# Moving the value projection behind the query-key transposes, and giving the self-attention output another PSUM bank, in a two-layer decoder kernel

## What is computed

```python
h = layernorm(x) * ln_g + ln_b                 # xn, then xT once it is transposed
q, k, v = h @ Wq.T, h @ Wk.T, h @ Wv.T         # 4 heads of 64
q, k = rmsnorm(q) * q_gamma, rmsnorm(k) * k_gamma
p = softmax(q @ k.T / 8)                       # per head
x1 = layernorm(layernorm(x) + (p @ v) @ Wo.T + bo)
```

## Time and profile before

| | |
|---|---|
| Median of 3 runs | 1514.06 us (1513.68 to 1515.25) |
| Profiled execution | 1514.06 us, span 1512.2 us |
| Mean granted clock of PE | 0.956 of full |
| Busy share of the span: PE, DVE, ACT, POOL | 90%, 73%, 62%, 55% |
| Self-attention stage (to slot 63) | about the first 160 us |
| Cross-attention stage | to about 650 us |

### The profile page before, as it was taken

One profiled execution on the slowest core, in us unless ns is written; L12 is line 12 of the kernel. 1 busy time (PEld: TensorE's weight loads), 2 busy tenths in 40 slices (PEclk: granted clock), 3 DMA queues, 4 the chain that ended last, 5 costly groups with the idle time before them and its releaser, 6 DMA issues.

```text
span 1512.2 us, 27707 instructions
## 1 busy us (share of the span) xinstructions
PE 1355.4 (90%) x9290; PEld 1093.8 (72%) x9290; DVE 1110.2 (73%) x2430; ACT 930.7 (62%) x2302; POOL 830.5 (55%) x866
## 2 busy tenths in 40 slices
PE   4888999999999999956999999878899998999991
PEld 4666777777777777645899999734556565899991
DVE  4898766666666766646688886389898996779935
ACT  4776565555655556534488884147788883548853
POOL 3675454444444444431688875138796885048850
PEclk9999999999999999975899999979999999999996
DMA  4100000000000000034566657674444340227784
GB/s 153 43 29 8 29 9 8 2 8 2 8 9 1 9 1 1 2 120 183 191 230 228 226 210 233 231 267 136 143 155 145 129 140 14 96 85 250 260 270 177
DMA packets 52942, 167.85 MB, mean 111 GB/s; under 512 B 13178, under 2 KB 22340, under 8 KB 44996
## 3 DMA queue, kind: packets, MB, share of 16 engines
q1 hardware_dynamic: 45316, 145.63, 27.3%
q0 software_dynamic: 7488, 20.46, 4.2%
HBM read 149.28 MB, written 16.78 MB: 110 GB/s over the span
## 4 chain that ended last, share of the span: by engine, by line
PE 34%; POOL 8%; DVE 7%; issue 4%; ACT 2%; DMA 1%; POOLq 0%; DVEq 0%; SPq 0%; ACTq 0%
PE m_ps L1756 10%; PE m_ps L1779 10%; POOL s_hc L2082 5%; PE m_ps L1753 2%; PE m_ps L1774 2%; PE s_yps L2517 2%; DVE s_h L2452 1%; PE m_ps L1736 1%; PE s_yps L2629 1%; DVE tokens L1624 1%; DMA table<-m_xn 1%; PE m_ps L1704 1%; ACT s_dps L2161 1%; PE m_ps L1660 1%; PE m_ps L1715 0%
## 5 line engine op out<-in xcount | busy, mean ns | idle before, releaser
L306 POOL TENSOR_TENSOR a_pexp<-a_pexp,a_rsum 128x384 f32<-128x384 f32 (+1 forms) x320 | 245.9, 787 | 289.7 <-DVE a_rsum L523 289.6
L396 ACT ACTIVATE a_pexp<-a_ps,a_nmax 128x384 f32<-128x384 f32 (+1 forms) x320 | 180.9, 566 | 175.8 <-DVE a_nmax L519 175.0
L519 DVE TENSOR_REDUCE a_nmax<-a_ps 128x1 f32<-128x384 f32 (+1 forms) x320 | 153.6, 521 | 61.5 <-PE a_ps L620 60.4
L2082 POOL TENSOR_TENSOR s_hc<-s_h,s_bc_rows 128x1024 f32<-128x1024 f32 x64 | 151.0, 2361 | 53.6 <-DVE s_h L2452 53.1
L1756 PE MATMUL m_ps<-m_xT,m_w1s 128*128 128x256 f32 x1032 | 155.1, 287 | 2.1 <-DVE m_xT L1509 2.1
L1779 PE MATMUL m_ps<-m_w2s,m_hs 128*128 128x256 f32 x1032 | 152.1, 283 | 0.0
L1103 POOL DMA_INDIRECT m_xrow<-table,m_row_from x78 | 83.6, 1072 | 118.9 <-DVE m_row_from L1451 85.7
L2452 DVE TENSOR_TENSOR_SCAN s_h<-s_dps,s_inp 128x512 f32<-128x512 f32 x128 | 148.8, 1203 | 0.0
L636 PE MATMUL a_ps<-a_ident,a_pexp 128*128 128x128 f32 x896 | 143.9, 273 | 3.6 <-ACT a_pT L255 3.0
L1756 PEld LDWEIGHTS m_ps<-m_xT,m_w1s 128*128 128x128 f32 x1032 | 137.0, 193 | 2.8 <-DVE m_xT L1509 2.5
L1779 PEld LDWEIGHTS m_ps<-m_w2s,m_hs 128*128 128x128 f32 x1032 | 135.6, 191 | 0.0
(11 more groups left out here) (442 smaller groups left out, 3562.9 us busy)
## 6 DMA issues: line engine op xcount, KB each, us to landing
s_bc_rows<-s_bc_table SPq DMA_DIRECT2D x64, 512.0 KB, 3.7
arrived<-in_down SPq DMA_DIRECT2D x29, 1024.0 KB, 8.1
arrived<-in_up SPq DMA_DIRECT2D x23, 1024.0 KB, 5.8
m_w<-in_up SPq DMA_DIRECT2D x16, 512.0 KB, 5.7
m_w<-in_down SPq DMA_DIRECT2D x16, 512.0 KB, 5.0
carried_up<-in_up SPq DMA_DIRECT2D x8, 512.0 KB, 5.9
carried_down<-in_down SPq DMA_DIRECT2D x8, 512.0 KB, 6.7
arrived<-results SPq DMA_DIRECT2D x3, 1024.0 KB, 8.5
```

What stands on the lines that cost most here:

```text
L306: nc.gpsimd.tensor_tensor(pexp[:, r, 0:n], pexp[:, r, 0:n], rsum[:, r:r + 1].to_broadcast([128, n]), ALU.mult).then_inc(normed, 1)
L396: nc.scalar.activation(pexp[:, r, 0:n], ps_s[score_bank(u)][:, 0:n], ACT.Exp, bias=nmax[:, r:r + 1], accum_out=sums[:, r:r + 1]).then_inc( ...
L519: nc.vector.tensor_reduce(nmax[:, u % RING:u % RING + 1], ps_s[score_bank(u)][:, 0:keys_of(u)], AX.X, ALU.max, negate=True).then_inc(maxed, 1)
L2082: nc.gpsimd.tensor_tensor(halves(hc[:, u % HC_RING, :]), halves(h[:, u % H_RING, :]), bc_rows[:, u % BC_RING, 1, :].unsqueeze(1).to_broadc ...
```

## The change

`vs` is put one slot later, behind `qkT1`, where it was ahead of `qkT0`. `oself` moves from bank 4, which it shared with `pv`, to bank 5, where `xnT` and `vs` are; bank 4 is left to `pv`.

```diff
@@ -135,9 +135,9 @@
             v = U0 * t
             put(v, "xnT", t + 2)
             put(v + 2, "oself", t - 2)
-            put(v + 4, "vs", t + 2)
             put(v + 4, "qkT0", t + 1)
             put(v + 5, "qkT1", t + 1)
+            put(v + 5, "vs", t + 2)
             put(v + 6, "qk0", t + 2)
             put(v + 7, "qk1", t + 2)
@@ -155,7 +155,7 @@
-        FIXED = {"qk0": 6, "qkT0": 6, "qk1": 7, "qkT1": 7, "xnT": 5, "vs": 5, "oself": LAST_PT_BANK, "pv": LAST_PT_BANK}
+        FIXED = {"qk0": 6, "qkT0": 6, "qk1": 7, "qkT1": 7, "xnT": 5, "vs": 5, "oself": 5, "pv": LAST_PT_BANK}
```

## The result

The changed kernel is slower. The medians are 1532.47 us against 1513.87 us of the kernel before, 18.6 us apart; the ratio over the executions is 1.0127 (95% interval 1.0113 to 1.0140), which is 19.2 us (17.1 to 21.2). A second comparison, on another chip, gave 1.0111 (1.0094 to 1.0129), 16.8 us. I had forecast 1528 us, 14 us slower. The direction was right and the size too small: scaled to the 1514.06 us of the first runs by the first ratio, the time is 1533.3 us, just past the upper end of my range (by the second it would be 1530.9, inside it).

What follows compares the result with a forecast made beforehand. DVE, in places PE, was taken to set the pace to about slot 48, PE after; 5.4 - 0.5 + 4.4 + 1.0 + 4.0 = 14.3 us on 1514.06 gave 1528 us, range 1517 to 1533.

Steps and rivals of the forecast that it cites:

- The clock: TensorE falls to 1.2 GHz when `vs`, scores and `qk0` run: 1.0 us in four of periods 0 to 4, 4.0 us.
- The move of `vs`: Behind `qkT1`, `vs` delays PE by 1.28 us: 0.51 us each in periods 2 to 4, 1.28 in the others, 5.4 us.
- half absorbed: Rival: slack behind `oself` or faster row operations behind the copy absorb half of the terms; 1519 us, chance 0.13.
- The start: In slot -4, `qkT0` first brings L464 sooner, but `vs` then stands ahead of `qk0`: a gain of 0.5 us.
- The bank: `oself` waits for ACT to drain `xnT`: 1.1 us in slots 18, 26, 34, 42 (4.4 us), plus 1.0 in slot 50.
- The clock stays: Rival: all waits as forecast in the periods, but no more falls of the clock than before; 1524 us, chance 0.23.
- nothing: Rival: the gain at L464 and the loss by bank 5 cancel, nothing measurable; 1514 us, chance 0.07.
- Faster: Rival: L464's wait goes at both `qkT` jobs and `vs` fits between `qkT1` and the copy L255; 1509 us, chance 0.07.

Runs made afterwards that it cites:

- move filled: Kernel before with only the move of `vs`, plus 16 unread identity transposes on PE ahead of `qkT0` in periods 0 to 5; ratio 1.0023 to before, 3.5 us.
- change filled: Changed kernel plus 16 unread identity transposes on PE ahead of `qkT0` in periods 0 to 5; ratio 1.0081 to the kernel before.
- half fill: Changed kernel plus 8 unread identity transposes ahead of `qkT0`, executed once; periods 0 to 5 took 14.87, 18.89, 20.28, 20.29, 18.79, 17.68 us.
- bank alone: Kernel before with only `oself` moved from bank 4 to bank 5, `vs` staying ahead of `qkT0`; ratio 1.0037 to before, 5.7 us.
- move alone: Kernel before with only `vs` moved behind `qkT1`, `oself` staying in bank 4; ratio 1.0086 to before, 13.1 us.

## Why the prediction was right in direction and short in size

The terms can be set against the periods. "Filled" is the run with 16 transposes; all numbers are us.

| | 0 | 1 | 2 | 3 | 4 | 5 | sum |
|---|---|---|---|---|---|---|---|
| move, forecast | 1.28 | 1.28 | 0.51 | 0.51 | 0.51 | 1.28 | 5.4 |
| move filled, less before | 1.82 | 1.15 | 0.56 | 0.34 | 0.44 | 0.53 | 4.8 |
| bank, forecast | - | - | 1.1 | 1.1 | 1.1 | 1.1 | 4.4 |
| change filled, less move filled | 0.05 | 0.02 | 0.75 | 1.09 | 1.11 | 0.58 | 3.6 |
| change, less change filled | 0.60 | 1.48 | 1.55 | 1.48 | 1.46 | 0.81 | 7.4 |

- **The clock (4.0 us).** This is the term that failed in size. The step was "over the twelve of `vs` that is 1.0 us", taken "for four of the periods 0 to 4". The last row shows 7.4 us in its place (6.9 at slot 48, 147.07 against 140.16, as the filled run started 0.5 us later). Periods 1 to 4 pay 1.46 to 1.55 us each (in period 1 although the filled run still had a low stretch there), not 1.0, since the low clock does not stop with `vs`: `vs` lost 1.1 us (2.49 against 1.39), and the rest of the 1.50 us between `qkT1` and `qk0` is in the transposes, the scores and what lies between. And it was paid in every period, also 0.8 us in period 5, which I had left out. In period 0 the full fill was itself in the way; with the half fill that period took 14.87 us, 1.98 less than in the changed kernel. Taken by that, the clock's part of period 0 is 2.0 us and the sum 8.8. My bound of 7.5 us holds the one sum and not the other.
- **The move of `vs` (5.4 us).** The mechanism is as told: the copy L255 waits 1.27 us for PE, and the next maxima carry what is left. The sizes are partly luck. Periods 2 to 4 measured 0.56, 0.34 and 0.44 for my 0.51, but my sentence that DVE's own work fits between the copy and the maxima was wrong. In the kernel before that work takes 97.89 - 94.39 = 3.50 us with no idle time in it; from 95.45 on it ends at 98.95, not by 98.40, and the period would have grown by 1.06 us. It came out near 0.5 because L493 shrank from 1.97 us to 0.73, and to 0.80 to 1.05 in the filled runs, where it met less of POOL's work or none. This is the mechanism that I had named for the rival "half absorbed". Period 5 paid 0.53 us, not 1.28. Period 0 paid 1.82 with the full fill, but the half fill left 0.49 (14.87 against 14.38), so the move without the clock is 3.5 to 4.8 us.
- **The start (-0.5 us).** Open. Period 0 began at 31.61 us before, at 31.88 and 32.40 in the two traces of the changed kernel, and at 33.88 with the bank alone, whose order up to there is that of before; the start scatters by more than the term. From slot -8 to period 0 it took 12.97 us before and 12.38 to 12.69 in the changed kernel, the move alone and the two filled ones, which would be the gain; but the runs with PE's old order took 11.5 us where the clock stayed full and 13.8 where it was low for longer (bank alone; the half fill, with the new order, also took 13.8). No run separates the two.
- **The bank (4.4 + 1.0 us).** Right in mechanism: `oself` waited 1.10 us where I had 1.24. The four slots cost 3.6 us by the table, less than 4.4, since in period 5 only 0.58 was on the path. From slot 48 to the first `qkT0` behind `k0` it is 156.82 - 147.07 = 9.75 us instead of 8.81, 0.94 against the 1.0 predicted. The 5.7 us timed for the bank alone hold some low clock too.
- **These together.** Without the clock I had 10.3 us. The filled changed kernel reaches slot 48 at 140.16, 9.2 us later than before, and with the 0.94 us behind it makes 10.1. That these agree so well is chance: a start 0.74 us later and period 0 too long in that run stand against the bank and period 5 too short.
- **The sum.** 10.1 + 6.9 = 17.0 us against 14.3, and 17.1 us is what the attention lost. Both comparisons of the times (16.8 and 19.2 us) agree with it within their intervals.
- **The rivals.** "The clock stays" falls, by every period of the trace. The advice of the Trainium skill (TensorE: Matmul & The Clock Gate, "Why this matters for your kernels"), which I had set beside my term, warns only of idle gaps longer than the ones here. The traces don't agree with that as a limit: behind gaps of 2.86 us in three periods, and behind two of three of 1.84 us, with shorter gaps beside them, the granted clock fell. "Half absorbed" and "nothing" fall with the table of periods, though part of what the first named, shorter row operations, did happen. "Faster" named a real gain, but its condition failed as the rows said: `vs` did not fit between `qkT1` and the copy.

## What to carry to other kernels

Work that stands ahead of a wait is free only there; moved behind the wait it is on the path, and the hole it leaves can cost more than the work. Here the work cost 3.5 to 4.8 us, and the clock of TensorE, which fell to 1.2 GHz behind the hole just when the moved work ran (2.49 us instead of 1.39), cost 7 to 9 us. When only the drain of a result is in the way of another, move the drain on its own engine and leave the product where it is. A PSUM bank shared by three jobs is a chain of waits: look up when the job before is drained, not only when its matmuls end. When you ask whether an engine's own work still fits behind a delay, add up its rows, and look what runs beside them: here two row operations of DVE took 1.97 us beside POOL and 0.73 without.

## What the runs showed that I had not expected

- The periods with a fall of the clock settled at 20.30, 20.29 and 20.36 us in one run and 20.30, 20.53 and 20.28 in another, with a stretch at low clock in each; without it they were 18.81 to 18.83 us.
- A gap of 1.84 us cost 1.5 us in periods 2 and 3 and nothing in period 4, in one and the same execution.
- The two halves of L493, 1.97 us in the kernel before, took 0.73 us in the changed one: a later start let them miss the work of POOL, and by the rows the period came out 0.62 us shorter for it.
- Work without any use (16 transposes a period) made the changed kernel some 4.5 to 7 us faster, and the move alone 6.5 us by the traces and 9.6 us by the times.
